# Expert stage: two slot tiles per DMA for the rows loaded and the results stored, the last tile by itself

## What is computed

```
scores = softmax(xf @ Wg.T);  weights, indices = top_k(scores, 2);  weights /= weights.sum(-1)
h1 = lora_in(xf, W1, b1, A1, B1);  h3 = lora_in(xf, W3, b3, A3, B3)
g  = silu(h1) * h3
y_e = lora_out(g, W2, b2, A2, B2)
y  = einsum('te,ted->td', gates, y_e)
x  = x + attention(xn) + y
```

## Time and profile before

| | us |
|---|---|
| median of 3 runs (1111.08 to 1111.59) | 1111.42 |
| the profiled execution, its own time | 1110.31 |
| its span | 1108.6 |
| PE busy | 1052.9 (95%) |
| DVE busy | 782.5 (71%) |
| ACT busy | 394.0 (36%) |
| POOL busy | 431.2 (39%) |

### The profile page before, as it was taken

One profiled execution on the slowest core, in us unless ns is written; L12 is line 12 of the kernel. 1 busy time (PEld: TensorE's weight loads), 2 busy tenths in 40 slices (PEclk: granted clock), 3 DMA queues, 4 the chain that ended last, 5 costly groups with the idle time before them and its releaser, 6 DMA issues.

```text
span 1108.6 us, 20431 instructions
## 1 busy us (share of the span) xinstructions
PE 1052.9 (95%) x6338; PEld 912.8 (82%) x6338; DVE 782.5 (71%) x1741; ACT 394.0 (36%) x770; POOL 431.2 (39%) x416
## 2 busy tenths in 40 slices
PE   5999999999999997999995999999999999999995
PEld 4899999999999996867764788888888888877774
DVE  5688787888788766766733777777777777764745
ACT  2636362555446463432210223233223223442310
POOL 2846453554446332037664100000001000088886
PEclk8999999999999999799997999999999999999998
DMA  9364572655367346325566446434255252365456
GB/s 271 101 207 130 183 249 102 192 154 198 140 193 203 135 144 190 95 79 182 186 204 196 167 162 219 157 101 153 92 194 186 63 191 59 98 113 86 67 95 142
DMA packets 113524, 168.61 MB, mean 152 GB/s; under 512 B 17040, under 2 KB 87312, under 8 KB 113296
## 3 DMA queue, kind: packets, MB, share of 16 engines
q1 hardware_dynamic: 93072, 120.09, 34.7%
q0 software_dynamic: 20352, 47.23, 15.4%
HBM read 96.14 MB, written 71.14 MB: 151 GB/s over the span
## 4 chain that ended last, share of the span: by engine, by line
PE 79%; DMA 6%; issue 6%; DVE 4%; POOL 3%; SPq 1%; DVEq 0%; ACT 0%; POOLq 0%
PE wide L549 19%; PE wide L1901 17%; PE bank L549 11%; PE bank L1901 9%; PE wide L1399 4%; PE bank L1926 3%; DMA ring<-xn_scratch 2%; DMA slot_rows_scratch<-ring,slot 2%; PE bank L1399 2%; POOL slot_rows_scratch L1348 2%; PE bank L640 1%; PE bank L1894 1%; PE wide L1459 1%; DMA lora<-in_expert_lora 1%; PE wide L1472 1%
## 5 line engine op out<-in xcount | busy, mean ns | idle before, releaser
L1901 PE MATMUL wide<-expert_ring,xsT 128*128 x642 | 170.5, 401 | 2.6 <-DVE xsT L1990 2.2
L1901 PEld LDWEIGHTS wide<-expert_ring,xsT 128*128 128x128 f32 x642 | 113.3, 188 | 23.1 <-issue 3.6
L1959 ACT ACTIVATE gsT<-bank 128x512 fp32r<-128x512 f32 x71 | 42.6, 601 | 242.2 <-PE bank L1926 242.2
L1784 POOL DMA_DIRECT2D expert_ring<-experts_scratch x24 | 17.3, 720 | 263.3 <-issue 137.4
L2002 DVE TENSOR_TENSOR slots_h<-wide,expert_bias 128x512 f32<-128x512 f32 x71 | 49.1, 692 | 67.6 <-PE wide L1901 67.4
L1348 POOL DMA_INDIRECT slot_rows_scratch<-ring,slot x64 | 66.6, 1041 | 70.4 <-DVE slot L1735 32.1
L532 POOL TENSOR_TENSOR folded_matrix<-fold,folded_matrix 128x512 fp32r<-128x512 f32 x48 | 64.3, 1347 | 42.3 <-ACT folded_matrix L726 39.5
L549 PE MATMUL wide<-xnT,w 128*128 128x512 f32 x234 | 60.3, 399 | 0.0
L944 DVE TENSOR_TENSOR hT<-hid,hT 128x512 fp32r<-128x512 f32 x64 | 55.4, 873 | 6.0 <-ACT hid L781 5.1
L1901 PEld LDWEIGHTS bank<-expert_ring,gsT 128*128 128x128 f32 x432 | 56.1, 189 | 3.5 <-issue 0.3
L549 PE MATMUL wide<-xnT,pT 128*128 128x512 f32 (+2 forms) x288 | 58.5, 348 | 0.0
(11 more groups left out here) (284 smaller groups left out, 2584.2 us busy)
## 6 DMA issues: line engine op xcount, KB each, us to landing
experts_scratch<-folded_matrix SPq DMA_DIRECT2D x24, 1024.0 KB, 5.1
expert_ring<-experts_scratch POOLq DMA_DIRECT2D x24, 1024.0 KB, 6.8
raw<-in_expert_weights SPq DMA_DIRECT2D x24, 512.0 KB, 7.2
xs_ring<-slot_rows_scratch SPq DMA_DIRECT2D x71, 128.5 KB, 2.1
slot_results_scratch<-ys_ring SPq DMA_DIRECT2D x71, 128.0 KB, 2.3
slot_rows_scratch<-zeros SPq DMA_DIRECT2D x23, 385.5 KB, 7.1
ring<-xn_scratch SPq DMA_DIRECT2D x16, 514.0 KB
xn_scratch<-u SPq DMA_DIRECT2D x16, 512.0 KB, 6.8
```

What stands on the lines that cost most here:

```text
L1901: ins = mm(o, parts[i], moving, start=(first and q == 0), stop=(last and q == 2))
L1959: return nc.scalar.activation(o, i, ACT.Copy)
```

## The change

Loads and stores of the expert stage go in pairs of tiles. `load_pair(sp, j)` loads tiles j and j + 1 (j is even) by one DMA into two neighbouring slots of `xs_ring`; one semaphore belongs to a pair of slots. The six first loads become three. Of the units MT only those of odd tiles and of the last one (tile 70) do something: MT of an odd tile j waits for `y_taken` at least j + 1, loads the pair (j + 5, j + 6) and stores the results of (j - 1, j) by one DMA. Tile 70 is loaded and stored alone. PE's wait in MR, DVE's wait before it writes `ys_ring`, and `results_stored` use the semaphores of the pairs. No buffer changes its size, and no instruction of PE, DVE, ACT or POOL is added, removed or moved.

```
-    x_in = [sem(f"slots_in{i}") for i in range(ROUND)]
-    y_out = [sem(f"slots_out{i}") for i in range(RING)]
+    x_in = [sem(f"slots_in{i}") for i in range(ROUND // 2)]
+    y_out = [sem(f"slots_out{i}") for i in range(RING // 2)]
...
-    xs_d = scr["xs"].rearrange("(s p) d -> s p d", p=P)
-    ys_d = scr["ys"].rearrange("(s p) d -> s p d", p=P)
+    xs_d = scr["xs"].rearrange("(s p) d -> p s d", p=P)
+    ys_d = scr["ys"].rearrange("(s p) d -> p s d", p=P)
...
+    def load_pair(sp, j):
+        n = min(2, SLOTS_T - j)
+        sp.dma_start(xs[:, j % ROUND:j % ROUND + n, :], xs_d[:, j:j + n, :]).then_inc(x_in[j % ROUND // 2], 16)
...
-                sp.dma_start(xs[:, j % ROUND, :], xs_d[j]).then_inc(x_in[j % ROUND], 16)
-            elif kind == "MT":
+                if j % 2 == 0:
+                    load_pair(sp, j)
+            elif kind == "MT" and (j % 2 or j == SLOTS_T - 1):
+                first, n = j - j % 2, j % 2 + 1
                 sp.wait_ge(y_taken, j + 1)
-                if j + ROUND < SLOTS_T:
-                    sp.dma_start(xs[:, j % ROUND, :], xs_d[j + ROUND]).then_inc(x_in[j % ROUND], 16)
-                sp.dma_start(ys_d[j], y[:, j % RING, :]).then_inc(y_out[j % RING], 16)
+                if first + ROUND < SLOTS_T:
+                    load_pair(sp, first + ROUND)
+                sp.dma_start(ys_d[:, first:first + n, :], y[:, first % RING:first % RING + n, :]
+                             ).then_inc(y_out[first % RING // 2], 16)
...
-            pe.wait_ge(x_in[j % ROUND], 16 * (j // ROUND + 1))
+            pe.wait_ge(x_in[j % ROUND // 2], 16 * (j // ROUND + 1))
...
-                dve.wait_ge(y_out[j % RING], 16 * (j // RING))
+                dve.wait_ge(y_out[j % RING // 2], 16 * (j // RING))
...
-        for k in range(RING):
-            engine.wait_ge(y_out[k], 16 * len(range(k, SLOTS_T, RING)))
+        for k in range(RING // 2):
+            engine.wait_ge(y_out[k], 16 * len(range(2 * k, SLOTS_T, RING)))
```

## The result

| | before | changed |
|---|---|---|
| median, us (7 runs each) | 1111.08 | 1115.18 |
| lowest and highest | 1108.85, 1112.54 | 1110.91, 1118.82 |
| the profiled execution, its span | 1110.31, 1108.6 | 1118.82, 1117.1 |

The ratio is 1.0043 (95% interval 1.0026 to 1.0059): slower by 4.8 us, between 2.9 and 6.6. The forecast was 1117.4, that is 6.0 us more, in a range of 1111.8 to 1122. The profiled execution of the changed kernel was its slowest run, so the difference of the two spans, 8.5 us, says too much: 2.65 us of it lie ahead of the first row load (issued at 605.82 instead of 603.17), where the change touches nothing.

What follows compares the result with a forecast made beforehand. PE, busy 340.78 of 343.00 us, was taken to bound the expert stage. Stalls of 5.75 us (5.2 + 0.55) and 0.2 us at the start made 6.0, added to 1111.42: 1117.4 us, range 1111.8 to 1122.

Steps and rivals of the forecast that it cites:

- Bound and mechanism: Expert stage: PE has no slack; the even tile's load lead falls from 10.8 to 5.9 us, later landings cost time.
- The term of 5.75 us: Pairs beside expert weight loads: 5.2 us at tiles 12, 34, 42, 50, plus 0.55 us beside the third weight part.
- the condition with which the prediction ends: Pairs in bursts: the forecast is wrong if the pair's second half does not queue as the store did.
- The second reckoning: Pairs in a burst: 4.4 us plus 2.9 us, landing about 7.2 us, 1.3 us late; four make 5.2 us.
- The third part, 0.55 us: Pairs beside an expert's third weight part: stalls of 0.41 us at tile 14 and 0.15 us at tile 44.
- Behind the three 1024 KB loads: Pair (18, 19), behind three loads at MU: 0.36 + 4.4 us is within 5.9, so it costs nothing.
- A free queue: Pairs off the bursts: a pair lands in about 2.4 us, 0.43 us more than a tile, and costs nothing.
- The start: First row load, now two tiles: transposes start 0.43 us later, partly hidden under DVE's chain; 0.2 us taken.
- SP, stores and the end: SP's issues, result stores and the kernel's end: 70 fewer DMAs and later stores cost or gain nothing.
- The first (in time in a burst): Four pairs in a burst: they land in time, as if the skill's formula held throughout; 1112.2 us, chance 0.23.
- The second (clock): After PE's stalls: the granted clock falls too, adding 4.2 us (1121.6) or 14.4 us (1131.8); chance 0.09.
- The third (backlog and size add up): Pairs in bursts: each takes the backlogged landing and 2.9 us more; 1129 us, or 1123 with half; chance 0.07.

Runs made afterwards that it cites:

- the 8 slots: The changed kernel with a ring of 8 row slots instead of 6, each further pair loaded two tiles earlier; 1.0001 of the kernel before.
- the small experts: The changed kernel loading only 64 of 1024 columns per weight part and 16 numbers per bias for the third to eighth expert; 1.0003 of the kernel before.
- the second profile: Profile of the unaltered changed kernel, run once more against the kernel before; 1115.29 us against 1111.02, ratio 1.0035.
- the run with the store first: The changed kernel with the pair's store issued ahead of the pair's load after an odd tile; 1.0167 of the kernel before.
- five slots: The kernel before, loads and stores of single tiles, with a ring of 5 row slots instead of 6; 1.0133 of the kernel before.

## Why the prediction was right, by its own steps

**Bound and mechanism.** PE bounds the stage, and the lead of the even tile falls from 10.8 to 5.9 us: shown, by the waits after, by the 8 slots that take them away and by the small experts that take them away. The loads, not the stores, carry it.

**The term of 5.75 us.** The profile shows 5.46 us in single stops, 5.63 in D; the second profile 3.9. The forecast of 1.85 + 1.85 + 1.35 + 0.15 us for tiles 12, 42, 34 and 50 met 1.62, 1.39, 0.99 and 0.49. But it was right for a partly wrong reason, and two errors cancelled. I let the pair's second half land where the next store had landed, up to 7.76 us after the issue; it lands after 5.8 to 6.9 us, 0.3 to 1.1 us sooner at each of the four. By the condition with which the prediction ends, that step failed. By the landings alone only 1.88 us of visible wait came, not the 5 to 6 us that I expected in PE's list of waits. The other 3.6 us are the fixed price of a stop, 0.77 us, which had no term in the sum (I wrote that each us of lateness is an us of the kernel), and for which the kernel before has no row: it has no stop in a steady tile. That the sum comes out near the measured time is luck.

**The second reckoning**, 4.4 us for an empty queue in a burst and 2.9 us for the second tile, came to 7.2 us. Neither part holds in the middle of a burst: single loads take 5.3 to 6.4 us there and a pair some tenths more. Both terms of it were mis-sized, and that the two ways met was no evidence.

**The third part, 0.55 us** (tiles 14 and 44): nothing. In the changed kernel the pair that brings tile 14 was issued at 675.14 and took 2.9 us. POOL had issued the third part 4.5 us ahead of it, at 670.62, where it had been 0.6 us ahead before. Two things moved them apart: the stop at tile 12 put the load 1.6 us later, and POOL issues the third part when the first two have landed, which was 12.0 us after their issue (658.59) instead of 14.2 (656.13). So a stop shifts the next meeting of load and burst, and my sum had priced each meeting as if the others had not happened.

**Behind the three 1024 KB loads**, tile 18: I wrote nothing, by 0.36 + 4.4 within 5.9. The pair took 6.2 us in the profile above and cost 0.97 us; in the second profile the excess there is 0.3 us, with the loads alone in pairs none. I had put 4.4 us, read off a single tile's store, which left a margin of 1.15 us; a pair needed 0.9 us more on a free queue already. The step that failed is that I gave such a margin a price of nothing. Tiles 22 and 36 had only 0.1 us by the same working (0.36 + 5.5 and 0.36 + 5.4 against 5.9) and got nothing too; they came through in both profiles, and the run with the store first shows how near tile 22 was.

**A free queue**: I gave a pair 2.4 us, 0.43 us more than a tile; it takes 2.9 us at 644 and 3.0 in the page's median. Without effect, the lead covers it. By the formula of the Trainium skill (DMA: Bandwidth & Descriptors, section on the anatomy of one DMA) for a DMA that POOL issues, 2.0 us and the bytes at 436 GB/s, an estimate gives 2.6 us for 257 KB. The trace agrees on the free queue within 0.3 us, for SP's DMA, and not in a burst, where the pair took 5.8 to 6.9 us; the rival by which that formula holds throughout falls there.

**The start**, 0.2 us: from the first issue to the transposes of tile 8 it is 44.17 us before and 44.30 after, 0.13 us more, though the first load landed 0.7 us later (2.7 us against 2.0). DVE's chain covered the rest, as said.

**SP, stores and the end**: no wait of DVE for a store after, and from tile 70 to the end of the span it is 158.8 us before and 158.9 after. Right.

**Rivals.** The first (in time in a burst) is nearer the truth than its chance said in one point: at some stops the pair missed by only 0.2 us. At tiles 12 and 18 of the second profile it did land in time, after 5.5 and 5.6 us. The second (clock) did not happen in the two profiles of the change, but its mechanism exists: it cost 1.5 us at two stops of the run with the store first, and 3.6 us at two stops with five slots. The third (backlog and size add up) did not show: no pair of the change took over 6.9 us, and in the middle of a burst even a store ahead of it added at most some tenths to that.

## What to carry to other kernels

Merging two loads of a ring costs the first of them one step of lead, and that is paid where the load is slowest, beside the other queue's bursts and behind large loads of its own queue, not at the median: compare the longest landing with the shortened lead, or add two slots. An engine that never stops can hide register loads that stand in its program; a stop uncovers them, so add a fixed price to each new stop, and put such reads ahead of the wait. When a constant of the ring is changed, look whether other DMAs of the same queue have moved: here two stores slipped into a burst. Fewer DMAs gave nothing here, since nobody waited for their issue or their fixed time.

## What the hardware showed that I had not expected

A stop of PE costs 0.77 us beyond its visible wait, 0.6 us of it by a register load behind the transposes and what hangs on it; even a load that landed 0.1 to 0.2 us ahead of the transposes (tile 50) left 0.49 us. Single 128.5 KB loads issued in the middle of a burst, with nothing of the tile before still under way, take 5.3 to 6.4 us, a merged one of twice the size only some tenths more. At the head of a burst 0.4 us of later issue and a store ahead took a pair from 2.9 to 8.3 us. And the granted clock fell to 0.62 over four us after a stop of 2.63 us and to 0.64 after one of 1.31 us, in a stage where PE had been busy throughout, but not after stops of 1.69 and 2.78 us; what decides that stays open. In both profiles of the changed kernel all stops after tile 0 were under 0.9 us, and the clock stayed up.
